# Taking the filler matmuls out of the TensorE stream of a four-stage vision tower

## The chip, the cores and the metric

The kernel runs on one core of one Trainium2 chip. The metric is the time of one execution on the device in microseconds (us); the median of the runs shown counts. A core has TensorE (PE, matrix products; its weight loads are listed as PEld), VectorE (DVE), ScalarE (ACT), GpSimd (POOL) and a queue of transfers issued by SyncE (SP). Engines work in parallel, each through its own list of instructions in order, and wait for each other by semaphores.

## The reference, cut to what matters

64 images of 3 x 224 x 224 are cut into 14 x 14 = 196 patches, and each patch becomes a token of 256 numbers. Four stages follow, each added to its input and then normalised over the 256 numbers.

```python
h = tok(x, W, b)                          # (64, 196, 256): patches times a matrix
h = layernorm(h + mamba(h))               # in-projection, 4 taps, x-projection, scan over tokens, out-projection
h = layernorm(h + rwkv_channel_mix(h))    # r, k, v products of h mixed with its previous token
h = layernorm(h + attention(h))           # 8 heads, leaky scores, softmax, gamma * out + x
h = layernorm(h + top2_moe(h))            # 8 experts, the two best gates of each token
```

Inside the second stage, for 512 channels and 16 states, the scan is `state[t] = dA[t] * state[t-1] + u[t] * B[t]` and the output is the sum over states of `state * C`. All is computed in 32-bit floats.

## The kernel before, in words

The kernel is a software pipeline over images. Work on one image is cut into pieces, and each piece has a slot number (the constants `AT_...`, lines 58 to 141) counted in units of a sixteenth of an image. One pass `step(b, par)` goes through 16 slots g; at each slot every engine does the pieces whose number is g modulo 16, for the image that is there at the time (`live`, line 168). So pieces of about eight images lie side by side at any time, and an image period is 16 slots. Each engine's own `step` function fixes the order within a slot. The order is written out by hand, and no planner changes it.

A slot has a group of the scan as its regular load. GpSimd makes `u * B` for four states (line 474), VectorE scans them in two halves (line 1105) with the decays that ScalarE makes by an exponential (line 907), GpSimd multiplies by C (line 484), and TensorE adds the four states into the bank YB by transposing them (`sum_states`, line 601). After four groups ScalarE drains columns 0 to 255 of YB into `ysb` (line 914). The products `X` go through a ring of six buffers.

Around that load lies the work of the other stages. What the prediction's steps touch:

- TensorE, `project_in` (line 578): the in-projection into the bank pair S, half of it for `z` (slot 20) and half for `xb` (slot -23).
- TensorE, `project_out` (lines 622 and 625), `queries_keys` (line 658), `scores` (line 670), `turn_probs` (line 680), `mix_values` (line 693): the out-projection and the attention.
- TensorE, `expert_pair` (line 721) with the bias row (line 727): two experts at a time, from the scaled inputs `hg` that VectorE makes (line 1221) into a ring of two buffers. The third scaling waits until the first pair is through.
- VectorE, `add_residual` (line 1230): adds the token's input to the experts' sum; it runs once per image.
- VectorE, `attended` (line 1164 and on) after each value product; the gated z (line 1095) and the gated x (line 1090), which free the bank pair S.
- ScalarE: drains of `ysb`, of the transposed probabilities `pT` (line 986), of queries and keys `qm`, `km` (lines 961, 963).
- GpSimd: the inverse deviations of the normalisations (lines 489 to 496).

Among these pieces TensorE also has filler work: `keep_busy(n)` (line 545) issues n products of the identity with a part of the in-projection's weights. They write to columns 256 to 451 of YB, which nothing drains. They wait for no semaphore and raise none. The tuples `AT_WARM` and `WARM` (lines 58 and 59) say at which slots they come and how many: four at slot 5, four at 8, four at 9, three at 12, two at 13, so 17 per image. In the trace each of the products is two records, because a product of 32-bit floats runs in two passes: 34 records per image, 2176 in all.

Of the kernel before, what the change touches and what calls it, by code (L numbers as in the profile page):

```python
# [11 lines left out]
P = 128  # L12
# [5 lines left out]
T = SIDE * SIDE  # L18
BLK = 2
TB = T // BLK  # L20
# [34 lines left out]

AT_WARM = (5, 8, 9, 12, 13,)
WARM = (4, 4, 4, 3, 2,)
AT_LOAD = -39  # L60
AT_PATCH = (-30, -29, -26,)
AT_PATCH_OUT = (-29, -28, -25,)
# [105 lines left out]
def live(b, par, g, slot):  # L168

    if (slot - g) % GROUPS:  # L170
        return ()
    s = image_of(b, slot)
    if isinstance(s, int) and not 0 <= s < IMAGES:
        return ()
    return ((s, (par - slot // GROUPS) % CYCLE),)
# [19 lines left out]
def vit_tower(nc, x, w_tok, b_tok, w_in, conv_w, conv_b, w_xproj, a_log, d_par, dt_w, dt_b, w_out, ln_g, ln_b,  # L195
              w_r, w_k, w_v, mu_r, mu_k, w_qk, b_q, b_k, w_vv, b_v, gamma, w_g, b_g, w_e, b_e,
              ident, q_mask, k_mask, rank_of, proj, gates, out):
    with ExitStack() as ctx:  # L198
        def sb(name, shape, dt=F32):
            return ctx.enter_context(nc.sbuf_tensor(name, shape, dt))  # L200

        def psum(name, shape):
            return ctx.enter_context(nc.psum_tensor(name, shape, F32))
# [7 lines left out]
        win = sb("win", [P, DC, 2 * INNER])  # L211
# [29 lines left out]
        idn = sb("idn", [P, P])  # L241
# [62 lines left out]
        YB = psum("YB", [P, 512])  # L304
# [232 lines left out]
        def _(pe):  # L537
            mm = nc.tensor.matmul
# [3 lines left out]
                after(pe, bank.drained, bank.count(name, s) - 1)  # L542
                return bank.tile

            def keep_busy(n):

                for _ in range(n):
                    mm(YB[0:TB, BLK * P:BLK * P + T], lhsT=idn[:, 0:TB], rhs=win[:, 0, 0:T], start=False, stop=False,  # L548
                       skip_group_check=True)

            def patches(s, part):

                o = free(f"patch{part}", s)
                if part == 0:
                    pe.wait_ge(x_landed, 16 * PATCH * (s + 1))
                for i, col in enumerate(range(QA * part, min(QA * (part + 1), SIDE))):
                    last = nc.tensor.transpose(o[:, i * PROWS:(i + 1) * PROWS], px[:, col, :, :].rearrange("r p w -> r (p w)"),
                                               idn[:PROWS, :PROWS])
                last.then_inc(where[f"patch{part}"].filled, 1)
# [46 lines left out]
            def turn_y(s):  # L606
                pe.wait_ge(normed["y"], s + 1)
                o = free("turn_y", s)
                for c in range(IC):
                    for k in range(BLK):  # L610
                        at = (c % 2) * T + k * TB
                        last = nc.tensor.transpose(o[:, c // 2, at:at + TB], ysb[:, k, c * P:(c + 1) * P],
                                                   idn[:TB, :TB])
                last.then_inc(S.filled, 1)
# [14 lines left out]
            def turn(s, name, src):  # L629
                o = free(name, s)  # L630
                for m in range(DC):
                    for k in range(BLK):
                        last = nc.tensor.transpose(o[:, m * T + k * TB:m * T + (k + 1) * TB],
                                                   src[:, k, m * P:(m + 1) * P], idn[:TB, :TB])
                last.then_inc(where[name].filled, 1)
# [61 lines left out]
            def gate(s, q):  # L697
                pe.wait_ge(where["h3T"].drained, where["h3T"].count("h3T", s))
                o = free("gate", s)
                for k in range(BLK):  # L700
                    for c in range(DC):
                        last = mm(o[0:TB, k * EXPERTS:(k + 1) * EXPERTS], lhsT=h3T[q % 2][:, c, k * TB:(k + 1) * TB],
                                  rhs=wg[:, c, :], start=(c == 0), stop=(c == DC - 1))
                last.then_inc(where["gate"].filled, 1)

            def turn_gates(s):
                pe.wait_ge(where["gate"].drained, where["gate"].count("gate", s))
                o = free("ws", s)
                for k in range(BLK):
                    last = nc.tensor.transpose(o[0:EXPERTS, k * TB:(k + 1) * TB], gw[:, k, :], idn[:TB, :TB])  # L710
                last.then_inc(where["ws"].filled, 1)
# [19 lines left out]
            def turn_moe(s):  # L731
                pe.wait_ge(accT_ready, s + 1)
                o = free("moeT", s)
                for k in range(BLK):
                    for m in range(DC):
                        last = nc.tensor.transpose(o[0:TB, k * D + m * P:k * D + (m + 1) * P],  # L736
                                                   accT[:, m, k * TB:(k + 1) * TB], idn[:])
                last.then_inc(where["moeT"].filled, 1)

            def step(b, par):  # L740
                for g in range(GROUPS):
                    def at(slot):
                        return live(b, par, g, slot)

                    for s, q in at(AT_WARM[0]):
                        keep_busy(WARM[0])
                    for s, q in at(AT_WARM[4]):
                        keep_busy(WARM[4])
                    for s, q in at(AT_H3T):
                        pe.wait_ge(normed["att"], s + 1)  # L750
                        turn(s, "h3T", h3)
                    for s, q in at(AT_WARM[1]):
                        keep_busy(WARM[1])
                    for s, q in at(AT_WARM[2]):
                        keep_busy(WARM[2])
                    for s, q in at(AT_H3T2):
                        turn(s, "h3T2", h3)
                    for s, q in at(AT_TURN_Y):
                        turn_y(s)
                    for s, q in at(AT_WS):  # L760
                        turn_gates(s)
                    for s, q in at(AT_GATE):
                        gate(s, q)
                    for s, q in at(AT_WARM[3]):
                        keep_busy(WARM[3])
                    for p in range(PAIRS):
                        for s, q in at(AT_PAIR[p]):
                            expert_pair(s, p)
                    for s, q in at(AT_MOE_T):
                        turn_moe(s)  # L770
                    for s, q in at(AT_EMBED):
                        embed(s)
                    for s, q in at(AT_V):
                        pe.wait_ge(ksq_ready, s + 1)
                        token_major(s, "v", ka, wv)
                    for part in range(3):
                        for s, q in at(AT_PATCH[part]):
                            patches(s, part)
                    for n in range(UNITS):
                        for s, q in at(AT_SCORES[n]):  # L780
                            scores(s, n)
                    for n in range(UNITS):
                        for s, q in at(AT_TURN_P[n]):
                            turn_probs(s, n)
                    for s, q in at(AT_RK):
                        pe.wait_ge(mix_step, 4 * (s + 1))
                        token_major(s, "r", xr, wr)
                        mix_keys(s)
                    for n in range(UNITS):
                        for s, q in at(AT_AV[n]):  # L790
                            mix_values(s, q, n)
                    for s, q in at(AT_H1T):
                        pe.wait_ge(where["out"].drained, where["out"].count("out", s))
                        turn(s, "h1T", h1)
                    for s, q in at(AT_QK):
                        queries_keys(s)
                    for k in range(GROUPS):
                        for s, q in at(k + 2):
                            sum_states(s, q, k)
                    for s, q in at(AT_Z):  # L800
                        project_in(s, hT[q], "z", IC)
                    for s, q in at(AT_XB):
                        pe.wait_ge(where["embed"].drained, where["embed"].count("embed", s))
                        project_in(s, hT[q], "xb", 0)
                    for s, q in at(AT_XPROJ):
                        xproj(s)
                    for s, q in at(AT_OUT):
                        project_out(s, q)
                    for s, q in at(AT_H2T):
                        pe.wait_ge(normed["ffn"], s + 1)  # L810
                        turn(s, "h2T", h2[q % 2])
                    for s, q in at(AT_VALUES):
                        token_major(s, "values", h2T, wvv)
# [568 lines left out]
```

## Time and profile before

| | us |
|---|---|
| median of the three runs | 5296.42 |
| range of the three runs | 5291.37 to 5298.24 |
| profiled execution, span from the first to the last instruction | 5291.6 |
| busy in the profiled execution: TensorE | 4820.6 |
| VectorE | 3739.1 |
| ScalarE | 3911.0 |
| GpSimd | 4452.7 |

The profile gives no other time for its execution than the span. It is read as follows: the busy time of an engine is the union of its instructions, and ends of TensorE's records are modelled, since products are pipelined. The granted clock of TensorE stands as a share of 2.4 GHz; it has two levels, 0.50 (1.2 GHz) and 1.00 (2.4 GHz), and a figure between them is a mean over a stretch that has both. In a timeline, consecutive records of one line are merged; a bracket tells how long the engine stood idle before the first of them, and what ended that.

### The profile page before, as it was taken

How to read it: one execution, taken by the hardware profiler on the slowest of the kernel's cores; microseconds unless marked ns; L12 is line 12 of the kernel's file. 1: busy time of each engine (PE TensorE's matmuls, PEld its weight loads, DVE VectorE, ACT ScalarE, POOL GpSimd, SP SyncE). 2: the span in 40 equal slices, each digit the busy share in tenths (PEclk: the TensorE clock that was granted, in tenths of full speed). 3: DMA queues.
4: the chain of work that ended last, by engine and by line, in shares of the span. 5: the costliest groups of instructions: out<-in, count | busy, mean ns of one | idle time of the engine just before them, and what ended most of it. 6: DMA issues, size and time to landing. Idle time of an engine off the chain costs nothing. (4 is left out here: it accounts for less than half of the span.)

```text
span 5291.6 us, 96290 instructions
## 1 busy us (share of the span) xinstructions
PE 4820.6 (91%) x33664; PEld 4234.3 (80%) x33664; DVE 3739.1 (71%) x7504; ACT 3911.0 (74%) x9282; POOL 4452.7 (84%) x3336
## 2 busy tenths in 40 slices
PE   4789999999999999999999999999999999999986
PEld 4678888888888888888888888888888888888776
DVE  3567777777777777777777777777777777777653
ACT  4687787787777787777777777787777777777751
POOL 4998898898898898898888888898898898898840
PEclk8899999999999999999999999999999999999986
DMA  4222222222222222222222222222222322322200
GB/s 96 60 54 71 57 61 72 57 62 72 61 61 68 59 66 66 64 63 64 67 60 64 68 59 64 67 61 64 71 59 61 71 59 61 75 58 58 66 16 25
DMA packets 730625, 329.04 MB, mean 62 GB/s; under 512 B 631542, under 2 KB 655392, under 8 KB 729888
## 3 DMA queue, kind: packets, MB, share of 16 engines
q1 hardware_dynamic: 730144, 322.89, 25.0%
q8 instruction: 269, 4.41, 0.3%
q14 instruction: 212, 1.74, 0.1%
HBM read 307.88 MB, written 14.90 MB: 61 GB/s over the span
## 5 line engine op out<-in xcount | busy, mean ns | idle before, releaser
L1105 DVE TENSOR_TENSOR_SCAN X<-dA,X 128x392 f32<-128x392 f32 x2048 | 1871.4, 955 | 844.9 <-POOL X L474 447.9
L474 POOL TENSOR_TENSOR X<-u,Bb 128x784 f32<-128x784 f32 x1024 | 1898.2, 1854 | 3.9 <-DMA Bb<-proj_rows 3.9
L484 POOL TENSOR_TENSOR X<-X,Cb 128x784 f32<-128x784 f32 x1024 | 1897.2, 1853 | 1.1 <-DVE X L1105 1.1
L907 ACT ACTIVATE dA<-dt,negA 128x195 f32<-128x195 f32 x4096 | 1511.6, 417 | 135.2 <-DVE X L1105 116.2
L601 PE MATMUL YB<-idn,X 128*98 128x128 f32 x8192 | 1106.7, 281 | 25.6 <-POOL X L484 25.4
L601 PEld LDWEIGHTS YB<-idn,X 128*98 128x98 f32 x8192 | 931.3, 132 | 62.9 <-POOL X L484 33.9
L721 PE MATMUL G<-hg,we 128*128 128x196 f32 x4096 | 727.8, 334 | 27.1 <-DVE hg L1221 27.1
L721 PEld LDWEIGHTS G<-hg,we 128*128 128x128 f32 x4096 | 694.9, 194 | 47.4 <-issue 40.8
L578 PE MATMUL SB<-hT,win 128*128 128x196 f32 x2048 | 375.3, 337 | 58.0 <-ACT pT L986 55.8
L548 PE MATMUL YB<-win,idn 128*98 128x196 f32 x2176 | 424.1, 335 | 0.0
L693 PEld LDWEIGHTS G<-vs,pT 98*98 98x98 f32 x4096 | 392.6, 171 | 36.2 <-issue 33.4
L693 PE MATMUL G<-vs,pT 98*98 98x33 f32 x4096 | 397.8, 253 | 21.0 <-DVE ob L1119 9.2
L578 PEld LDWEIGHTS SB<-hT,win 128*128 128x128 f32 x2048 | 340.1, 192 | 84.5 <-issue 66.2
L978 ACT ACTIVATE pr<-pr,nmx 98x196 f32<-98x196 f32 x1024 | 382.6, 447 | 8.2 <-DVE nmx L1152 2.6
L1082 DVE SCALAR_TENSOR_TENSOR xbs<-SB,cw,xbs 128x195 f32<-128x195 f32 (+2 forms) x768 | 266.8, 409 | 166.9 <-ACT xbs L851 162.7
L489 POOL TENSOR_TENSOR veps_att<-mv_att,epsc 98x2 f32<-98x2 f32 x64 | 12.6, 197 | 435.0 <-DVE mv_att L1114 435.0
L1221 DVE TENSOR_TENSOR hg<-G,Gb 128x784 f32<-128x784 f32 x256 | 241.4, 963 | 179.8 <-PE G L721 167.1
L914 ACT ACTIVATE ysb<-YB 98x256 f32<-98x256 f32 x256 | 96.1, 375 | 355.6 <-PE YB L601 345.4
L548 PEld LDWEIGHTS YB<-win,idn 128*98 128x98 f32 x2176 | 350.1, 169 | 3.2
L670 PE MATMUL SB<-km,qm 32*98 32x392 f32 x1024 | 235.0, 533 | 104.8 <-DVE xbs L1090 100.3
L569 PE MATMUL G<-patT,wtok 128*128 128x196 f32 x1536 | 277.2, 338 | 4.3 <-ACT patT L833 4.2
L680 PE MATMUL SB<-idn,pr 98*98 98x98 f32 x2048 | 219.7, 251 | 66.2 <-DVE zs L1095 62.5
(149 smaller groups left out, 7609.0 us busy)
## 6 DMA issues: line engine op xcount, KB each, us to landing
Bb<-proj_rows SPq DMA_DIRECT2D x256, 392.0 KB, 5.2
Cb<-proj_rows SPq DMA_DIRECT2D x256, 392.0 KB, 4.1
Gb<-gate_rows SPq DMA_DIRECT2D x64, 784.0 KB, 5.5
px<-in_x SPq DMA_DIRECT2D x1024, 36.8 KB
out<-ob SPq DMA_DIRECT2D x64, 196.0 KB
dtin<-proj_rows SPq DMA_DIRECT2D x64, 98.0 KB, 2.8
we<-in_w_e SPq DMA_DIRECT2D x1, 2048.0 KB
proj_rows<-pj SPq DMA_DIRECT2D x64, 25.3 KB
```

The source lines that it names most:

```text
L474: tt(X[(GROUPS * s + g) % RING][:], u[q % 2][:, c:c + 1, :].broadcast_to([P, NG, T]), Bb[:, NG * ng:NG * (ng + 1), :], ALU.mult).then_inc( ...
L484: tt(t[:], t[:], Cb[:, n0:n0 + NG, :], ALU.mult).then_inc(prod_ready, 1)
L548: mm(YB[0:TB, BLK * P:BLK * P + T], lhsT=idn[:, 0:TB], rhs=win[:, 0, 0:T], start=False, stop=False, skip_group_check=True)
L569: last = mm(o[:, m * T:(m + 1) * T], lhsT=wtok[:, k, m * P:(m + 1) * P], rhs=patT[:, half * COLORS + c, :], start=(k == 0), stop=(k == KP ...
L578: last = mm(o[:, j // 2, (j % 2) * T:(j % 2 + 1) * T], lhsT=win[:, k, m * P:(m + 1) * P], rhs=src[:, k, :], start=(k == 0), stop=(k == DC ...
L601: last = mm(YB[0:TB, k * P:(k + 1) * P], lhsT=X[(GROUPS * s + g) % RING][:, j, k * TB:(k + 1) * TB], rhs=idn[:], is_transpose=True, start= ...
L693: last = mm(o[0:TB, j * (DV + 1):(j + 1) * (DV + 1)], lhsT=pT[:, j // 2, at:at + TB], rhs=vs[q % 2][:, k, h0 + j, :], start=(k == 0), stop ...
L721: last = mm(o[:, m * T:(m + 1) * T], lhsT=we[:, k, at:at + P], rhs=hg[p % GRING][:, e, k, :], start=(p == 0 and e == 0 and k == 0 and m == 0),
L907: last = go(dA[i % DRING][:, j, 1:T], dt_[q % 2][:, c, 1:T], ACT.Exp, scale=negA[:, c, n:n + 1])
L978: last = go(pr[i % PRING][:, j, :], pr[i % PRING][:, j, :], ACT.Exp, bias=nmx[i % PRING][:, j:j + 1])
L1082: last = v.scalar_tensor_tensor(out=xbs[:, c, k:], in0=S.tile[:, c // 2, at:at + T - k], scalar=cw[:, c, TAPS - 1 - k:TAPS - k], in1=xbs[: ...
L1105: v.tensor_tensor_scan(t, dA[i % DRING].rearrange("p n t -> p (n t)"), t, 0.0, ALU.mult, ALU.add).then_inc(scan_done, 1)
```

## The change

The filler products go: their function, their five calls and the two tuples. Every other piece keeps its slot and its place in the order of its engine.

```diff
-AT_WARM = (5, 8, 9, 12, 13,)
-WARM = (4, 4, 4, 3, 2,)
...
-            def keep_busy(n):
-
-                for _ in range(n):
-                    mm(YB[0:TB, BLK * P:BLK * P + T], lhsT=idn[:, 0:TB], rhs=win[:, 0, 0:T], start=False, stop=False,
-                       skip_group_check=True)
-
...
-                    for s, q in at(AT_WARM[0]):
-                        keep_busy(WARM[0])
-                    for s, q in at(AT_WARM[4]):
-                        keep_busy(WARM[4])
                     for s, q in at(AT_H3T):
                         pe.wait_ge(normed["att"], s + 1)
                         turn(s, "h3T", h3)
-                    for s, q in at(AT_WARM[1]):
-                        keep_busy(WARM[1])
-                    for s, q in at(AT_WARM[2]):
-                        keep_busy(WARM[2])
...
                     for s, q in at(AT_GATE):
                         gate(s, q)
-                    for s, q in at(AT_WARM[3]):
-                        keep_busy(WARM[3])
```

## Rows read from the trace of the kernel before

**Rows 1.** The page: busy us, share and instructions of engines; granted clock in 40 slices.

```profile
PE 4820.6 (91%) x33664; PEld 4234.3 (80%) x33664; DVE 3739.1 (71%) x7504; ACT 3911.0 (74%) x9282; POOL 4452.7 (84%) x3336
...
PEclk8899999999999999999999999999999999999986
```

**Rows 2.** Instructions of L1230 in four stretches: duration ns, first and last start us.

```profile
L1230 DVE TENSOR_TENSOR accT<-G,h3T x5: 554/555/556, 1062.6 to 1377.5; 128x392 f32<-128x392 f32 x5
...
L1230 DVE TENSOR_TENSOR accT<-G,h3T x58: 553/555/557, 429.0 to 4940.6; 128x392 f32<-128x392 f32 x58
...
L1230 DVE TENSOR_TENSOR accT<-G,h3T x2: 554/555/556, 1456.3 to 1536.7; 128x392 f32<-128x392 f32 x2
...
L1230 DVE TENSOR_TENSOR accT<-G,h3T x2: 554/555/556, 1536.7 to 1616.3; 128x392 f32<-128x392 f32 x2
```

**Rows 3.** Stretches: us; busy us of PE, PEld, DVE, ACT, POOL; PEclk, DMA share, GB/s.

```profile
1117.00:1196.00 79.00, 73.49 (x531) 64.56 (x530) 58.55 (x118) 61.24 (x147) 69.80 (x53) 1.00 0.26 64
...
485.00:4909.00 4424.00, 4142.31 (x29392) 3647.41 (x29393) 3256.97 (x6532) 3408.79 (x8110) 3887.75 (x2908) 0.99 0.26 64
```

**Rows 4.** Groups by line: busy us, mean ns of one, idle us before them.

```profile
L548 PE MATMUL YB<-win,idn 128*98 128x196 f32 x2176 | 424.1, 335 | 0.0
```

**Rows 5.** Timeline of PE, one undisturbed image: start us, us, what, idle before.

```profile
1200.70 0.83 PE L548 MATMUL YB<-win,idn 128*98 128x196 f32 x4
1201.95 5.54 PE L721 MATMUL G<-hg,we 128*128 128x196 f32 x32 [0.43 <-DVE hg L1221]
...
1240.25 1.49 PE L548 MATMUL YB<-win,idn 128*98 128x196 f32 x8
...
1243.14 0.85 PE L680 MATMUL SB<-idn,pr 98*98 98x98 f32 x8 [0.96 <-DVE zs L1095]
...
1255.43 1.49 PE L548 MATMUL YB<-win,idn 128*98 128x196 f32 x8
1256.76 1.50 PE L693 MATMUL G<-vs,pT 98*98 98x33 f32 x16
...
1259.32 1.49 PE L548 MATMUL YB<-win,idn 128*98 128x196 f32 x8
...
1262.80 2.89 PE L578 MATMUL SB<-hT,win 128*128 128x196 f32 x16 [1.11 <-ACT pT L986]
...
1274.54 1.16 PE L548 MATMUL YB<-win,idn 128*98 128x196 f32 x6
1277.34 0.90 PE L670 MATMUL SB<-km,qm 32*98 32x392 f32 x4 [1.65 <-DVE xbs L1090]
```

**Rows 6.** Timelines of VectorE, GpSimd and ScalarE, same image: waits for TensorE and behind.

```profile
1204.88 0.97 DVE L1221 TENSOR_TENSOR hg<-G,Gb 128x784 f32<-128x784 f32 x1 [2.19 <-PE G L721]
...
1206.99 0.20 POOL L489 TENSOR_TENSOR veps_att<-mv_att,epsc 98x2 f32<-98x2 f32 x1 [6.08 <-DVE mv_att L1114]
...
1245.43 0.18 DVE L1164 RECIPROCAL rg<-G 98x4 f32<-98x4 f32 x1 [0.42 <-PE G L693]
...
1272.37 0.92 ACT L961 ACTIVATE qm<-G,bqm,qmask 96x196 f32<-96x196 f32 x2 [4.14 <-PE G L658]
```

**Rows 7.** Two stretches (columns of rows 3), and the timeline of PE in the second.

```profile
1481.80:1488.60 6.80, 6.72 (x34) 5.92 (x33) 6.07 (x26) 6.26 (x17) 6.72 (x6) 0.50 0.02 5
...
1594.40:1597.80 3.40, 3.40 (x18) 2.77 (x15) 3.33 (x7) 1.80 (x5) 1.82 (x2) 0.51 0.36 118
...
1597.37 1.08 PE L548 MATMUL YB<-win,idn 128*98 128x196 f32 x4
1598.28 4.97 PE L721 MATMUL G<-hg,we 128*128 128x196 f32 x29
```

**Rows 8.** Timeline of PE in the last images, and the stretch around (columns of rows 3).

```profile
5116.20 1.51 PE L680 MATMUL SB<-idn,pr 98*98 98x98 f32 x8
5119.21 2.85 PE L693 MATMUL G<-vs,pT 98*98 98x33 f32 x16 [1.50 <-DVE ob L1119]
...
5115.00:5125.00 10.00, 7.59 (x36) 6.53 (x37) 3.40 (x14) 2.87 (x6) 2.69 (x3) 0.50 0.30 102
```

## The prediction, made before the change was run

> **What bounds the kernel now.** First the page's engine line and its clock line [rows 1]: TensorE (PE) is busy for 91% of the span, more than any other engine, and its granted clock reads 9 tenths or more from the third of the 40 slices to the third from the end. The share alone would say that PE is the bound and that less work on it is time won. So the next look is at one instruction that runs once per image, the residual add of line 1230 [rows 2]. Its starts give the length of an image: (1377.5 - 1062.6) / 4 = 78.73 us in an undisturbed stretch, and (4940.6 - 429.0) / 57 = 79.15 us over all 57 steady intervals. A whole image is 57 times in the sum below; the difference of 0.42 us per image, 24 us in all, is to be explained too.
>
> In the undisturbed stretch the clock is 1.00, that is 2.4 GHz, and PE is busy 73.5 of 79 us [rows 3]. The fillers take 424.1 us of the span and no idle time stands before them [rows 4]. What PE does behind each filler is in its timeline over one image [rows 5]. There are five groups: 4 records at 1200.70, 8 at 1240.25, 8 at 1255.43, 8 at 1259.32 and 6 at 1274.54. The reader is to see the idle time in brackets: after the fillers, PE stands still and waits for another engine, 0.96 us before L680 (VectorE), 1.11 before L578 (ScalarE), 1.65 before L670 (VectorE) and 0.43 before L721 (VectorE). No filler ends a wait of anybody; at 2.4 GHz each lies beside a wait that PE would have anyway.
>
> The image's length is set by a chain that changes engines. Its PE links are those for which another engine stands idle [rows 6]: the first expert pair (VectorE waits 2.19 us for L721, and GpSimd 6.08 us for the statistics behind that), the probability transposes and value products (VectorE waits for L693), and the long run from L578 at 1262.80 to the query projection (ScalarE waits 4.14 us for L658, until 1272.37: 9.5 us of PE). So PE's idle stretches and PE's chain links lie side by side: every link starts just after one of the four waits of rows 5.
>
> **What the change removes.** Five groups per image, 34 records. One record steps by 166 ns: the group of 8 at 1255.43 is followed by the next work at 1256.76 [rows 5], 1.33 us later. That is 34 x 0.166 = 5.6 us of PE time per image, and I cost it at zero gain: the waits on ScalarE and VectorE that follow hide it, and those engines don't wait for a filler. The same removal lengthens PE's idle time by what stood in front of each wait: before L680 from 0.96 to about 2.3 us, before L578 from 1.11 to 3.8 us (two groups, less what the work between them can use), before L670 from 1.65 to 2.65, before L721 from 0.43 to 1.1. Nothing else is removed: no wait, no semaphore, no DMA; the queues of SP and GpSimd are untouched, since the fillers carry no increment and write columns 256 to 451 of YB, which no drain reads.
>
> **What it costs.** The clock falls to 1.2 GHz behind such idle stretches already, fillers and all [rows 7]: in 1481.8 to 1488.6 it is 0.50 (behind the wait before L680), in 1594.4 to 1597.8 0.51 (behind the wait before L670). These falls come in some images only. The image from 1536.7 to 1616.3, with only the second of them, took 79.6 us, 0.9 more than the undisturbed one; the one from 1456.3 to 1536.7, with falls at both places, 80.4, so 1.7 more [rows 2]. The average over all images is the 0.42. With the idle stretches 1.0 to 2.7 us longer, I expect a fall in nearly every image at each of three places:
>
> - Place 1, L680 and L693 behind the wait for VectorE. In the last images, where the clock was 0.50, the transposes took 1.51 us and the products 2.85 [rows 8], against 0.85 and 1.50 at 2.4 GHz [rows 5]. All of it low costs 0.66 + 1.35 = 2.0 us, a fall that starts behind it nothing. I take the middle, 1.0.
> - Place 2, L578 and what follows, 9.5 us of dense chain work. Rows before show no fall here. The bounds are 0 (the fall ends before 1262.80) and half of a low stretch of 6.8 us, 3.4; the short low stretch of rows 7 (3.4 us) at half speed costs 1.7. I take 1.7, since the work is dense and a fall may start inside the wait.
> - Place 3, L670 to the first expert pair. In the fall of 1594.4 four filler records take 0.91 us [rows 7] instead of 4 x 0.166 = 0.66, after other slowed work, and L721 starts late. Measured: 0.9 per image [rows 2]. Lower bound 0 (the filler's own time goes), upper bound the whole first pair at half speed: half of 5.54 us [rows 5], 2.8. I take 0.9, the nearest row.
>
> Sum 3.6 us per image; with a fall nine times in ten at each, 3.24. Of this 0.42 is paid already: 2.8 x 57 = 160 us. The start and the drain already run at a lower clock [rows 1] and get no term. The profiled execution spans 5291.6 us, at the low end of the runs shown (5291.4 to 5298.2, median 5296.4), so nothing large lies around it and 5 us are added to come to the median: 5291.6 + 160 + 5 = **5457 us**.
>
> The Trainium skill, "TensorE: Matmul & The Clock Gate", section Terms, prices time at the low clock as that time times one minus the granted share, so half of it. The trace disagrees for this kernel: the image that starts at 1456.3 was low for 6.8 us at place 1 [rows 7] and fell at place 3 as well, 10.2 us if that fall is as long as the one of 1594.4, which gives 5.1 us, and the image was 1.7 longer, because much of the low time lay beside other engines' work. By that rule three low stretches of 3.4 us would make 5.1 us per image.
>
> **Rivals.**
> (a) Only the two places that already fall do so, now in every image; place 2 keeps its clock. For: no row shows a fall there. Against: its idle stretch becomes the longest of all. 1.0 + 0.9 - 0.42 = 1.48, times 57: 84 us, so 5380 us.
> (b) The clock holds about as it does now, and the change does nothing. For: PE remains busy for about 68 of 79 us, and the undisturbed stretch holds 1.00 [rows 3] with waits of up to 1.65 us in it [rows 5]. Against: the falls of rows 7 came behind waits that the fillers still kept short. 5296 us, up to 5349 if the falls become a few more: 53 us, 0.9 per image, is place 3 alone in every image. The Trainium skill's same page, Part 1, says that the ramp penalty is under 1% of a typical kernel's span; by that, too, the change would stay under 5349 us. The trace so far agrees (24 us of 5292), but in a kernel with the fillers in.
> (c) Faster: the fillers themselves are what a fall costs. Mechanism: at 1.2 GHz the filler group at place 3 stands between L601 and L721; it begins at 1597.37 and L721 at 1598.28, 0.91 us later [rows 7], about the 0.9 that the image lost. Without it L721 starts on time, and if the falls don't become more frequent, up to 24 us come back: 5273 us. It decides while falls at place 2 (1.7 us each) come in fewer than 24 / 1.7 = 14 of the 57 images; below 8 of them the gain is over 0.2%. Against: the longer idle stretches before that place.
> (d) Every low stretch is paid in full, as chain work is dense at all three places and the clock needs as long to come back as before. 3 x 1.7 - 0.42 = 4.7, times 57: 267 us, so 5563 us. For: with fillers gone the cover of rows 5 is thin. Against: the 1.7 us that 10.2 low ones cost. By the rule of the skill's section Terms this would be the case.
>
> **How the numbers follow.** Forecast (three places, most images, 5381 to 5540) 0.67; (a) 0.14; (b) 0.08, of which 0.05 ends within the bound and 0.03 above it; (c) 0.04; (d) 0.07. About 0.2%, 10.6 us, is what a measurement of this kernel can tell from no change. Faster 0.04, the same 0.05, slower 0.67 + 0.14 + 0.03 + 0.07 = 0.91. The range takes in (a) with some of its spread and ends just short of (d): 5360 to 5550 us. The bounds of the places alone (0 to 2.0, 0 to 3.4, 0 to 2.8) would reach from no cost to 8.2 us per image; falls at the outer ends of all three at once I leave out.
>
> **What would show it.** Right: line 548 is gone; the residual add comes every 81 to 83 us instead of 78.7; the steady granted clock falls from 0.99 to about 0.9 to 0.95; L578, L693 and L721 show records near double length in most images; the idle time before L670 and L578 is longer in full-clock images; ScalarE waits longer than 4.14 us for L658 in a good part of the images. Each place is right if its own fall is there and the engine behind it waits longer by its term. Wrong: the interval stays at 78.7 to 79.2 with the clock at 0.99, (b); falls at places 1 and 3 only, (a); falls as now but no lost 0.9 at place 3, (c); an interval over 83.5, (d). Should the clock fall and the interval stay, the chain as I read it is wrong.

## The result, and the profile after

| | before | after |
|---|---|---|
| median, us | 5296.39 | 5461.04 |
| range of four runs, us | 5291.37 to 5298.24 | 5456.63 to 5464.29 |
| span of the profiled execution, us | 5291.6 | 5454.8 |

The ratio of after to before is 1.0312, with a 95% interval of 1.0297 to 1.0326: the change costs 165 us. The prediction was 5457 us.

Lines move up in the changed file: L578 is L570 after, L601 is L593, L622 is L614, L658 is L650, L670 is L662, L680 is L672, L693 is L685, L721 is L713, L961 is L943, L1230 is L1212.

First the page of the changed kernel, its engine line and its clock line, which answer to [rows 1].

```profile
PE 4681.1 (86%) x31488; PEld 4110.7 (75%) x31488; DVE 3741.5 (69%) x7504; ACT 3915.2 (72%) x9282; POOL 4447.5 (82%) x3336
...
PEclk7889999999999999999999999999999999999987
```

TensorE lost 2176 records and 139.5 us of busy time, and the kernel is longer. At one digit the clock line shows almost nothing of the cause. The residual add shows it, over all steady images and over four of them (answers to [rows 2]).

```profile
L1212 DVE TENSOR_TENSOR accT<-G,h3T x58: 552/556/558, 433.7 to 5103.0; 128x392 f32<-128x392 f32 x58
...
L1212 DVE TENSOR_TENSOR accT<-G,h3T x5: 552/555/558, 1089.0 to 1416.7; 128x392 f32<-128x392 f32 x5
```

(5103.0 - 433.7) / 57 = 81.92 us per image, against 79.15, and (1416.7 - 1089.0) / 4 = 81.93 in the sample. Before, 39 of the 57 images had no fall of the clock and took some 78.7 us, and the others up to 80.8; now every image has a fall, and 45 of the 57 lie within 0.1 us of 81.92. 57 x 2.77 = 158 us of the 163 us by which the span grew lie here; 4.7 us come before the first of these adds (433.7 against 429.0).

Then stretches of the changed kernel, with the columns of [rows 3]: the steady part, the two stretches of one image in which the clock was low, and the one around L662 and L713.

```profile
485.00:5070.00 4585.00, 4030.33 (x27541) 3550.08 (x27540) 3265.05 (x6548) 3415.11 (x8115) 3886.31 (x2910) 0.94 0.25 61
...
2015.30:2018.60 3.30, 3.30 (x21) 3.15 (x19) 2.69 (x15) 2.84 (x7) 3.16 (x4) 0.50 0.01 2
2032.30:2039.10 6.80, 6.06 (x18) 5.92 (x19) 3.13 (x6) 4.17 (x11) 6.80 (x5) 0.50 0.79 85
2047.40:2059.20 11.80, 8.06 (x54) 7.10 (x53) 7.89 (x16) 5.37 (x14) 5.16 (x5) 1.00 0.20 68
```

The timeline of TensorE in that image (answers to [rows 5]) tells what ran there.

```profile
2013.17 0.85 PE L672 MATMUL SB<-idn,pr 98*98 98x98 f32 x8 [2.29 <-DVE zs L1077]
2013.86 1.50 PE L685 MATMUL G<-vs,pT 98*98 98x33 f32 x16
2015.19 1.87 PE L593 MATMUL YB<-idn,X 128*98 128x128 f32 x8
2016.85 1.51 PE L604 MATMUL SB<-idn,ysb 98*128 98x98 f32 x8
...
2029.14 0.53 PE L625 MATMUL G<-idn,h 98*128 98x98 f32 x4 [0.98 <-ACT wsT L1016]
...
2033.04 5.57 PE L570 MATMUL SB<-hT,win 128*128 128x196 f32 x16 [2.49 <-ACT pT L968]
2038.40 2.28 PE L614 MATMUL G<-wout,y 128*98 128x256 f32 x8
...
2044.01 1.55 PE L650 MATMUL G<-h2T,wqk 128*96 128x196 f32 x8
...
2050.56 0.90 PE L662 MATMUL SB<-km,qm 32*98 32x392 f32 x4 [2.64 <-DVE xbs L1072]
...
2053.92 5.54 PE L713 MATMUL G<-hg,we 128*128 128x196 f32 x32 [1.09 <-DVE hg L1203]
```

Four things are to be seen. The waits grew (2.29, 2.49, 2.64 and 1.09 us, against 0.96, 1.11, 1.65 and 0.43), at places 1 and 3 by what the fillers had filled; before L570 only by 1.38 us, and another 0.98 stands before L625. At place 1 the transposes and the value products still run at 2.4 GHz (0.85 and 1.50 us), and the short fall hits the work behind them, L593 and L604. At place 2 the whole projection L570 takes 5.57 us instead of 2.89. At place 3, where the wait is the longest in this list, nothing falls: L713 takes 5.54 us as before.

Over the 57 images, place 1 falls in all, place 2 in 55 and place 3 in 2. One of the two images without a fall at place 2, by the residual add and the projection:

```profile
L1212 DVE TENSOR_TENSOR accT<-G,h3T x2: 557/557/557, 2402.7 to 2481.6; 128x392 f32<-128x392 f32 x2
...
2445.58 2.89 PE L570 MATMUL SB<-hT,win 128*128 128x196 f32 x16 [1.93 <-ACT pT L968]
```

Its clock is low at place 1 alone, for 6.8 us; its projection takes 2.89 us, and the image 78.9. So in one and the same kernel an image with the fall at place 2 is 3.0 us longer than one without it.

Last the waits of other engines in the image of the long timeline above (timelines of VectorE, GpSimd and ScalarE, answers to [rows 6]).

```profile
2056.85 0.97 DVE L1203 TENSOR_TENSOR hg<-G,Gb 128x784 f32<-128x784 f32 x1 [2.19 <-PE G L713]
...
2058.96 0.19 POOL L487 TENSOR_TENSOR veps_att<-mv_att,epsc 98x2 f32<-98x2 f32 x1 [6.64 <-DVE mv_att L1096]
...
2045.59 0.91 ACT L943 ACTIVATE qm<-G,bqm,qmask 96x196 f32<-96x196 f32 x2 [5.13 <-PE G L650]
```

VectorE waits for the expert pair exactly as long as before; ScalarE waits 1 us longer for the query projection.

### The profile page after: what moved, and what is told of

The parts are those of the page before. It is cut to its first block and busy times, and to the rows that moved or that the text cites. A ratio compares the mean times of both kernels' runs of the same rounds, so it can differ in the third digit from the quotient of the medians.

```text
span 5454.8 us, 91938 instructions
## 1 busy us (share of the span) xinstructions
PE 4681.1 (86%) x31488; PEld 4110.7 (75%) x31488; DVE 3741.5 (69%) x7504; ACT 3915.2 (72%) x9282; POOL 4447.5 (82%) x3336
## 5 line engine op out<-in xcount | busy, mean ns | idle before, releaser
L593 PE MATMUL YB<-idn,X 128*98 128x128 f32 x8192 | 1137.2, 286 | 27.6 <-POOL X L482 27.6
L593 PEld LDWEIGHTS YB<-idn,X 128*98 128x98 f32 x8192 | 952.0, 134 | 63.2 <-POOL X L482 35.7
L713 PE MATMUL G<-hg,we 128*128 128x196 f32 x4096 | 729.8, 335 | 73.0 <-DVE hg L1203 73.0
L713 PEld LDWEIGHTS G<-hg,we 128*128 128x128 f32 x4096 | 693.7, 194 | 92.5 <-DVE att L1151 81.3
L570 PE MATMUL SB<-hT,win 128*128 128x196 f32 x2048 | 526.0, 429 | 150.3 <-ACT pT L968 148.1
L570 PEld LDWEIGHTS SB<-hT,win 128*128 128x128 f32 x2048 | 478.0, 255 | 178.3 <-issue 160.0
L685 PE MATMUL G<-vs,pT 98*98 98x33 f32 x4096 | 402.1, 254 | 23.6 <-DVE ob L1101 12.1
L685 PEld LDWEIGHTS G<-vs,pT 98*98 98x98 f32 x4096 | 392.8, 173 | 38.8 <-issue 35.9
L662 PE MATMUL SB<-km,qm 32*98 32x392 f32 x1024 | 232.4, 528 | 165.0 <-DVE xbs L1072 160.0
L672 PE MATMUL SB<-idn,pr 98*98 98x98 f32 x2048 | 219.5, 251 | 147.2 <-DVE zs L1077 143.6
L672 PEld LDWEIGHTS SB<-idn,pr 98*98 98x98 f32 x2048 | 188.2, 129 | 167.0 <-issue 163.4
L943 ACT ACTIVATE qm<-G,bqm,qmask 96x196 f32<-96x196 f32 x128 | 58.4, 505 | 325.4 <-PE G L650 325.4
```

What stands on the lines that cost most here:

```text
L570: last = mm(o[:, j // 2, (j % 2) * T:(j % 2 + 1) * T], lhsT=win[:, k, m * P:(m + 1) * P], rhs=src[:, k, :], start=(k == 0), stop=(k == DC ...
L593: last = mm(YB[0:TB, k * P:(k + 1) * P], lhsT=X[(GROUPS * s + g) % RING][:, j, k * TB:(k + 1) * TB], rhs=idn[:], is_transpose=True, start= ...
L672: last = nc.tensor.transpose(o[0:TB, j // 2, at:at + TB], pr[(UNITS * s + n) % PRING][:, j, k * TB:(k + 1) * TB], idn[:TB, :TB])
L685: last = mm(o[0:TB, j * (DV + 1):(j + 1) * (DV + 1)], lhsT=pT[:, j // 2, at:at + TB], rhs=vs[q % 2][:, k, h0 + j, :], start=(k == 0), stop ...
L713: last = mm(o[:, m * T:(m + 1) * T], lhsT=we[:, k, at:at + P], rhs=hg[p % GRING][:, e, k, :], start=(p == 0 and e == 0 and k == 0 and m == 0),
```

## The experiments

Image lengths below are differences of the residual add's starts in each run's own trace, over 57 steady images where no stretch is named. Falls are counted in the same images: a fall is a stretch in which the clock is 0.50.

**Fillers at place 2 only.** The slots are 5, 8, 9, 12 and 13.

```diff
-WARM = (4, 4, 4, 3, 2,)
+WARM = (0, 4, 4, 0, 0,)
```

> Fillers only at slots 8 and 9, ahead of place 2 (the xb projection, L578 and on); none at slots 5, 12, 13. After the change each image had a long low stretch over the xb projection and a short one behind place 1, and none at place 3, at 81.92 us per image. Theory A (the cost is the clock at place 2): the projection stays at 2.4 GHz, most of the 165 us is back, and what is left is at place 1, 79 to 80 us per image: 5300 to 5370 us. Rival B (the three places share the cost, as the prediction had it; place 3 was spared only because the fall at place 2 shifted the image): falls at places 1 and 3 come back, 80.5 to 81.5 us per image: 5390 to 5450 us. Rival C (the fillers help by their time in PE's order, not by the clock): two of five groups back, 5395 us, with no link to the granted clock.

Measured: 5441.98 us, ratio 1.0276 (1.0260 to 1.0291), steady clock 0.93. Theory A falls and B holds: the place that carried the whole loss in the changed kernel is covered again, and only 19 us come back. The loss moved. The timeline of TensorE in this run:

```profile
3180.96 0.90 PE L670 MATMUL SB<-km,qm 32*98 32x392 f32 x4 [2.65 <-DVE xbs L1090]
...
3184.32 8.13 PE L721 MATMUL G<-hg,we 128*128 128x196 f32 x32 [0.76 <-DVE hg L1221]
```

A stretch of that time with the columns of [rows 3], its clock 0.52:

```profile
3182.50:3189.40 6.90, 6.14 (x23) 5.74 (x22) 2.48 (x6) 3.31 (x9) 0.57 (x1) 0.52 0.17 52
```

And the residual add over 11 images:

```profile
L1230 DVE TENSOR_TENSOR accT<-G,h3T x12: 555/556/558, 2795.5 to 3696.6; 128x392 f32<-128x392 f32 x12
```

Now place 3 falls, in 49 of the 57 images, beside place 1 in all of them: the two expert pairs take 8.13 us instead of 5.54. The wait before it is 2.65 us, the same as the 2.64 of the changed kernel, where the clock stayed at 1.00. So the length of the wait alone doesn't decide. The image is (3696.6 - 2795.5) / 11 = 81.92 us in this stretch, the length of the changed kernel, with the long fall at another place; over all 57 images it is 81.48.

**No fillers at place 2.**

```diff
-WARM = (4, 4, 4, 3, 2,)
+WARM = (4, 0, 0, 3, 2,)
```

> Fillers at slots 5, 12 and 13 as before, none at slots 8 and 9. Theory A: the xb projection runs low in nearly every image and the time is near that of the changed kernel, 5410 to 5465 us. Rival B: only place 2's own share is paid, 1.7 us per image by the prediction, 5296 + 97 = 5393 us or less. Rival C: three of five groups kept, 5365 us.

Measured: 5447.48 us, ratio 1.0287 (1.0271 to 1.0302), 81.65 us per image. Here theory A's number comes out and B's does not. Its timeline of TensorE shows the same long fall as the changed kernel has, and the wait at place 3 as in the kernel before:

```profile
2927.00 5.56 PE L578 MATMUL SB<-hT,win 128*128 128x196 f32 x16 [2.50 <-ACT pT L986]
...
2944.49 0.90 PE L670 MATMUL SB<-km,qm 32*98 32x392 f32 x4 [1.65 <-DVE xbs L1090]
...
2947.85 5.54 PE L721 MATMUL G<-hg,we 128*128 128x196 f32 x32 [0.43 <-DVE hg L1221]
```

Place 2 falls in 54 of the 57 images; place 1 falls in 37 and place 3 in 15, though their fillers are there. With the run before: opening place 2 costs 152 us, opening places 1 and 3 costs 147, opening all three 165. The losses don't add.

**Fillers over 8 partitions.**

```diff
-mm(YB[0:TB, BLK * P:BLK * P + T], lhsT=idn[:, 0:TB], rhs=win[:, 0, 0:T], start=False, stop=False,
+mm(YB[0:TB, BLK * P:BLK * P + T], lhsT=idn[0:8, 0:TB], rhs=win[0:8, 0, 0:T], start=False, stop=False,
```

> All fillers stay in their slots with the same count, output and length (196 columns, 98 output rows), but multiply over 8 partitions instead of 128. Theory A (clock): PE is busy as before, record for record, at equal clock; if the short products do as much for the clock as the full ones, 5296 us, and if they do little, the clock falls as in the changed kernel and the time is 5400 to 5500 us; either way time and granted clock go together. Rival C (their time in PE's order helps): 5296 us whatever the clock is.

Measured: 5652.54 us, ratio 1.0674 (1.0656 to 1.0692), 85.18 us per image, steady clock 0.90. The fillers' place in TensorE's order is the same as before, and the kernel is the slowest of all, so it isn't their time in the order that helps; rival C is out. From this run, the timeline of TensorE in one image:

```profile
3042.01 2.93 PE L548 MATMUL YB<-win,idn 8*98 8x196 f32 x8
...
3046.60 4.37 PE L578 MATMUL SB<-hT,win 128*128 128x196 f32 x16
...
3065.97 1.62 PE L548 MATMUL YB<-win,idn 8*98 8x196 f32 x4
3067.51 8.57 PE L721 MATMUL G<-hg,we 128*128 128x196 f32 x32
```

The stretch of this image, with the columns of [rows 3]:

```profile
3000.70:3088.50 87.80, 85.16 (x528) 74.32 (x526) 58.41 (x119) 61.09 (x146) 69.72 (x53) 0.86 0.24 58
```

With these fillers TensorE is busy for 85.16 of 87.8 us and still the clock is 0.86; and a group that takes 1.49 us at full clock takes 2.93 and then stands in front of chain work. That fits the 191 us more than with no fillers at all: where fillers don't hold the clock, they are ordinary work at half speed. How much of the 191 us it accounts for, no run shows.

**Every group doubled.**

```diff
-WARM = (4, 4, 4, 3, 2,)
+WARM = (8, 8, 8, 6, 4,)
```

> Every filler group doubled. By the prediction's reading the groups cost nothing because PE waits behind them: 0.96 us before L680, 1.11 before L578, 1.65 before L670, 0.43 before L721 at full clock. Doubling adds 1.33, 2.66, 1.00 and 0.66 us there, so it overruns by 0.4 + 1.5 + 0 + 0.2 = 2.1 us per image and ends the falls (0.42): 5296 + 57 x (2.1 - 0.42) = 5392 us, with clock 1.00 in the steady part. Rival (fillers were on the chain all along): doubling costs all of their 5.6 us per image, 5296 + 320 = 5616 us. Rival (much more slack than read): 5270 us.

Measured: 5352.50 us, ratio 1.0109 (1.0094 to 1.0124), steady clock 1.00, no low stretch in 57 images, 80.21 us per image: 1.5 us of overrun where 2.1 were expected, so the time lies 40 us under the 5392 of the expectation. The slack is where it was read. Of the groups by line of this run, the idle time before L578 and L680 (58.0 and 66.2 us in the kernel before) has nearly gone:

```profile
L578 PE MATMUL SB<-hT,win 128*128 128x196 f32 x2048 | 368.3, 333 | 3.7 <-ACT hT L842 1.7 <-ACT pT L986 1.3
...
L680 PE MATMUL SB<-idn,pr 98*98 98x98 f32 x2048 | 218.2, 250 | 6.0 <-ACT pr L971 2.7 <-DVE zs L1095 2.3 <-ACT pT L986 0.8
```

**More fillers at places 1 and 3 only.**

```diff
-WARM = (4, 4, 4, 3, 2,)
+WARM = (6, 4, 4, 6, 2,)
```

> Against the kernel before: six fillers instead of four at slot 5 (ahead of L680) and six instead of three at slot 12 (ahead of L670); 0.66 and 1.0 us more of PE per image, into waits of 0.96 and 1.65 us. Theory (a fall of the clock comes behind the idle stretches, and fillers within the wait are free): no fall in the steady part, every image 78.7 us as in the undisturbed stretch, 5296 - 24 = 5272 us. Rival (longer fillers sit on the chain): 57 x 1.66 = 95 us more, 5390 us, or something between. Rival (0.42 per image is not the clock): 5296 us.

Measured: 5266.51 us, ratio 0.9950 (0.9937 to 0.9963), 78.77 us per image. The theory's number was 5272. This version beats both kernels, by 28 us and 195 us. The residual add over the steady images:

```profile
L1230 DVE TENSOR_TENSOR accT<-G,h3T x58: 554/556/558, 425.7 to 4915.3; 128x392 f32<-128x392 f32 x58
```

The steady stretch, with the columns of [rows 3]:

```profile
485.00:4880.00 4395.00, 4176.90 (x29913) 3679.37 (x29911) 3254.59 (x6525) 3403.44 (x8100) 3878.71 (x2903) 1.00 0.26 64
```

The longer group at slot 5 and the wait behind it, from the timeline of TensorE:

```profile
1233.47 2.15 PE L548 MATMUL YB<-win,idn 128*98 128x196 f32 x12
1236.37 0.85 PE L680 MATMUL SB<-idn,pr 98*98 98x98 f32 x8 [0.31 <-DVE zs L1095]
```

The longer group leaves 0.31 us of the 0.96, and the clock of the steady part is 1.00: none of the 57 images has a fall. So the 0.42 us per image of the kernel before were falls, and covered waits cost nothing.

**Chain work added, with and without falls.** In the kernel with more fillers and in the changed kernel, one operation of GpSimd whose result nobody reads, behind the statistics of the attention norm; a second version for the changed kernel is smaller.

```diff
                 if n in shift:
                     pool.wait_ge(rstd_step[n], steps * (s + 1))
                     tt(shift[n][:], shift[n][:], rstd[n][:], ALU.mult).then_inc(shifted[n], 1)
+                if n == "att":
+                    tt(pad[:], bv[:], bv[:], ALU.add)
```

In the smaller version the line is `tt(pad[:, 0:2], bv[:, 0:2], bv[:, 0:2], ALU.add)`. From the groups by line of GpSimd, the changed kernel with the larger operation (which takes 614 ns in the kernel with more fillers, too) and with the smaller:

```profile
L497 POOL TENSOR_TENSOR pad<-bv 98x256 f32<-98x256 f32 x64 | 39.3, 614 | 0.0
```

```profile
L497 POOL TENSOR_TENSOR pad<-bv 98x2 f32<-98x2 f32 x64 | 12.4, 193 | 0.0
```

> The kernel with more fillers, and one added product-free GpSimd operation per image (98 x 256 numbers, about 0.6 us by the 392-wide one at 0.84) right behind the statistics of the attention norm, on the chain. Without falls the image has to grow by its whole length: 78.7 + 0.6 = 79.3 us, 57 x 0.6 = 34 us more than the kernel with more fillers, 5306 us. If GpSimd is not on the chain there: no difference.

Measured: 5306.80 us, 40.3 more than without the operation; 64 x 0.614 = 39.3. No image has a fall. The operation is on the chain, and where no clock falls the chain takes it in full.

> The changed kernel with the same added GpSimd operation. Theory E (in the changed kernel the image length is held by the falls: a longer image moves the next fall against the work, and the falls give way): the image stays at 81.9 us, 5461 us, within 8 us, although 0.6 us of chain work was added. Rival S (the length is a sum of prices): 82.5 us per image, 5461 + 34 = 5495 us.

Measured: 5502.82 us, 41.8 more than the changed kernel. Theory E falls in this form: the 0.61 us are paid. But the images are no longer even. The residual add over one image each, at two places of this run:

```profile
L1215 DVE TENSOR_TENSOR accT<-G,h3T x2: 555/556/556, 3243.5 to 3330.1; 128x392 f32<-128x392 f32 x2
...
L1215 DVE TENSOR_TENSOR accT<-G,h3T x2: 556/556/557, 3494.4 to 3574.8; 128x392 f32<-128x392 f32 x2
```

That is 86.6 us and 80.4 us, in sequences that partly repeat, with 82.72 on average: two or three falls per image, at places that change from image to image.

> The changed kernel with a smaller added GpSimd operation at the same place (98 x 2 numbers, about 0.2 us by the lines of the inverse deviations). With 0.61 us the images lost their even length. Theory E in a weaker form (the falls give way for a small shift): 81.9 us per image as before, 5461 us within 5. Rival S: 57 x 0.2 = 11 us more, 5472 us or more, and uneven images if the falls lose their place.

Measured: 5458.69 us, 2.4 less than the changed kernel at a spread of some 4, although 57 x 0.193 = 11 us of chain work was added. The residual add over five images of this run:

```profile
L1215 DVE TENSOR_TENSOR accT<-G,h3T x6: 554/555/557, 683.5 to 1093.1; 128x392 f32<-128x392 f32 x6
```

(1093.1 - 683.5) / 5 = 81.92 us. Of the 57 images 38 lie within 0.1 us of that, the others between 79.0 and 84.7, and the mean is 81.95. Where the 0.19 us went, the trace shows in a later image of even length (1994.3 to 2076.2):

```profile
2037.37 5.56 PE L573 MATMUL SB<-hT,win 128*128 128x196 f32 x16 [2.50 <-ACT pT L971]
2042.72 2.02 PE L617 MATMUL G<-wout,y 128*98 128x256 f32 x8
...
2048.08 1.55 PE L653 MATMUL G<-h2T,wqk 128*96 128x196 f32 x8
```

From the start of the projection to the end of L653 it is 2048.08 + 1.55 - 2037.37 = 12.26 us, where the changed kernel takes 12.52 (L650 there): L617 at first takes 2.02 us instead of 2.28, so the fall takes less of the work. The rest of the image is longer by as much, the operation included. So this shift was absorbed in most images, and the larger one was not. It is one run of each size; how the falls find their place, and why the larger shift breaks the even length, stays open.

**Fillers as transposes.**

```diff
-WARM = (4, 4, 4, 3, 2,)
+WARM = (6, 6, 6, 5, 3,)
...
-mm(YB[0:TB, BLK * P:BLK * P + T], lhsT=idn[:, 0:TB], rhs=win[:, 0, 0:T], start=False, stop=False,
+mm(YB[0:TB, BLK * P:BLK * P + P], lhsT=idn[:, 0:TB], rhs=idn[:], is_transpose=True, start=False, stop=False,
```

> Fillers of the kernel before as transposes: the identity turned, 128 columns each, 6, 6, 6, 5 and 3 of them, so about the same columns per group (768 for 784, 640 for 588, 384 for 392). Theory (what holds the clock is array work of any kind over all partitions): 5296 us, clock 0.97. Rival (a transpose does not count for the clock, as the Trainium skill, TensorE: Matmul & The Clock Gate, Part 4, has it): falls as with no fillers or with short ones, 5460 to 5650 us, clock 0.92 or less.

Measured: 5330.27 us, ratio 1.0058 (1.0038 to 1.0078), steady clock 0.98, 79.48 us per image. The five runs are uneven: two at 5310.5 us and three at 5330 to 5336, and the profile, with its clock and its image length, is of one of the former. The result lies between, much nearer the first: 36 us over the kernel before, where no fillers cost 165. But the groups are not as long as the expectation made them. In the trace a product of a filler is two records and a transpose one (1664 for 64 images with 26 transposes):

```profile
L548 PE MATMUL YB<-idn 128*98 128x128 f32 x1664 | 246.9, 282 | 0.0
```

```profile
1240.92 0.82 PE L548 MATMUL YB<-idn 128*98 128x128 f32 x6
...
1243.79 0.85 PE L680 MATMUL SB<-idn,pr 98*98 98x98 f32 x8 [1.62 <-DVE zs L1095]
```

A group takes 0.82 us instead of 1.49, and the wait behind it is 1.62 us instead of 0.96. The Trainium skill's page "TensorE: Matmul & The Clock Gate", Part 4, says that a transpose doesn't count as busy in the same way for the clock. This run disagrees in the main: with groups of transposes of about half the length, place 2 falls in none of the 57 images and 19 have no fall at all, where without fillers place 2 fell in 55 and every image had a fall. Whether a transpose does less for the clock than a product of the same length isn't parted here from the shorter groups: either can be what the 36 us are.

**One place opened at a time.**

```diff
-WARM = (4, 4, 4, 3, 2,)
+WARM = (0, 4, 4, 3, 2,)
```

> The kernel before without the four fillers at slot 5, ahead of L680 (place 1); all other fillers stay. In the runs so far the kernels with falls in every image all came to 81.5 to 81.9 us per image, whichever places fell, and one place was enough when it was place 2. Theory M (prices of falls don't add; one open place brings most of the loss): over 5400 us. Rival S (each place has a price of its own; place 1's is the smallest, 0.2 to 1.2 us per image): 5300 to 5360 us.

Measured: 5357.94 us, ratio 1.0116 (1.0099 to 1.0133), 80.27 us per image, clock 0.96. (The kernel with fillers over 8 partitions, at 85.18 us, does not fit the 81.5 to 81.9 of this expectation.) In 25 of the 57 images the only fall is one of 6.8 us at place 1, and they take some 80.3 us; in 29 place 3 falls too, though it has its fillers. An image of the first kind:

```profile
L1230 DVE TENSOR_TENSOR accT<-G,h3T x2: 554/555/556, 995.3 to 1075.7; 128x392 f32<-128x392 f32 x2
...
1019.19 2.77 PE L693 MATMUL G<-vs,pT 98*98 98x33 f32 x16
```

The image takes 80.4 us. Here the fall begins 23.6 us behind the residual add, over the value products, and costs 1.6 us; in the image of 78.9 us of the changed kernel it began 25.6 us behind it, after those products, was as long, and cost 0.2. So what a fall costs depends on the work that it meets.

```diff
-WARM = (4, 4, 4, 3, 2,)
+WARM = (4, 4, 4, 0, 0,)
```

> The kernel before without the fillers at slots 12 and 13, around L670 and ahead of the first expert pair (place 3); all other fillers stay. Theory M: over 5400 us. Rival S: 0.9 us per image by the prediction, less what is paid now, 5296 + 57 x 0.5 = 5325 us, and at most 5296 + 57 x 2.4 = 5433 us with the whole first pair low.

Measured: 5366.89 us, ratio 1.0116 (1.0077 to 1.0156), clock 0.95. Theory M falls in both: a single open place costs 61 or 70 us, where place 2 costs 152. Rival S gives the size for place 1 (within its range) and is low for place 3 (70 against 29, within its bound of 137). One run of four of the last kernel took 5323.75 us and three 5364 to 5370; the trace of one of the slower ones suggests why: the residual add over five early and ten later images.

```profile
L1230 DVE TENSOR_TENSOR accT<-G,h3T x6: 553/554/556, 670.7 to 1080.2; 128x392 f32<-128x392 f32 x6
...
L1230 DVE TENSOR_TENSOR accT<-G,h3T x11: 554/555/557, 2864.3 to 3661.9; 128x392 f32<-128x392 f32 x11
```

The images are (1080.2 - 670.7) / 5 = 81.90 us first and (3661.9 - 2864.3) / 10 = 79.76 later, of one and the same program: two patterns of falls within one execution. That the run of 5323.75 us had more of the second is not shown, since it has no trace.

## Why the prediction was right, and which of its steps were not

**The chain and the zero gain: right.** Fillers inside a wait are free: the version with more fillers loses nothing by them, and doubling all groups costs 1.5 us per image, once the waits are overrun. That the chain runs through L578 to L658 shows directly. L658 in the undisturbed image of [rows 5]:

```profile
1270.78 1.55 PE L658 MATMUL G<-h2T,wqk 128*96 128x196 f32 x8
```

From the start of the projection to the end of L658 it was 1270.78 + 1.55 - 1262.80 = 9.53 us, and it is 2044.01 + 1.55 - 2033.04 = 12.52 after. That is 2.99 of the 3.19 us by which an image exceeds the undisturbed 78.73. The other 0.2 lies between the residual add and the projection (42.9 us for 42.7), and nothing lies behind L658.

**The kind of cost: right.** The clock falls behind the lengthened waits and the chain pays. The fillers over 8 partitions rule out the other reading, that they help by their time.

**The sum by places: wrong in its parts.** The working gave 1.0 + 1.7 + 0.9 = 3.6 us, nine tenths of it 3.24; the image grew by 3.19. Place 2 was mis-sized: its low stretch is 6.8 us, not 3.4, the projection alone costs 5.57 - 2.89 = 2.68, and with L614 the place costs 2.99 where 1.7 was taken (the bound given was 3.4). The wait before it became 2.49 us, not the 3.8 that the prediction read. Place 1 has its fall in every image, but behind the chain's link, so it costs 0.2 where 1.0 was taken. The trace before had that price: the image from 2961.7 to 3040.6 has a fall at place 1 alone, for 3.4 us, and takes 78.9 us.

```profile
L1230 DVE TENSOR_TENSOR accT<-G,h3T x2: 555/556/556, 2961.7 to 3040.6; 128x392 f32<-128x392 f32 x2
```

Place 3 costs next to nothing where 0.9 was taken, since it falls in 2 of 57 images. The start, which got no term, cost 4.7 us. The errors of the places cancel (0.2 + 2.99 for 3.24), and that the time came within 4 us is luck in good part.

**The step that failed** is "a fall in nearly every image at each of three places": it treated the falls as independent. They aren't: with place 2 covered and the others open, place 3 falls and the kernel takes nearly as long (5442 us); with only place 3 open it costs 70 us. Whether a place falls depends on more than its wait, as 2.64 and 2.65 us show, with the clock at 1.00 in one kernel and a fall in the other. What else decides it was not isolated.

**The rivals.** (a), falls at places 1 and 3 only, is contradicted: place 2 falls in 55 of 57 images and place 3 in 2. (b) is contradicted. The Trainium skill's "TensorE: Matmul & The Clock Gate", Part 1, gives its 1% for the ramp, that is the warm-up of a kernel. Taken for falls in the steady part, as the prediction took it, it fits the kernel with its fillers (24 of 5292 us) and not the one without (165 of 5296 us, 3.1%). (c), faster, is contradicted: it asked for falls at place 2 in fewer than 14 images, and there were 55. That fillers at half clock can stand in front of chain work shows in another kernel, the one over 8 partitions. (d), every low stretch paid in full, is contradicted: an image of the changed kernel has low stretches of 3.4 and 6.8 us, and the first costs 0.2 us, since it meets little chain work; 3.19 us are paid for both. By the Trainium skill's "TensorE: Matmul & The Clock Gate", section Terms, they would cost 5.1 us.

**What the prediction wanted to see.** The interval of 81 to 83 us and the clock of 0.9 to 0.95 came (81.92 and 0.94), so did the double length of L578 and ScalarE's longer wait (5.13 for 4.14 us); the double length of L693 and L721 didn't come (1.50 and 5.54 us in the image shown, as before).

## What to carry to other kernels

Work on an engine with idle stretches isn't priced by its busy time: look at what it stands in front of, and then at the granted clock in a stretch, not at its mean (one digit hid a loss of 3%). Cover waits that lie ahead of chain work with array work that fits inside them, and check by the image length, not by the fillers' count: two groups made a little longer gave 28 us, doubling all of them cost 57. When several places can lose the clock, take them out one by one and all together, since what one costs depends on the others, and on the work that its fall meets.

## What was not expected of the hardware

Kernels with falls at different places come to the same 81.92 us, within 0.1, in most of their images: the changed one in 45 of 57 and the one with the small added operation in 38 (falls at places 1 and 2), the one with fillers at place 2 alone in 38 (places 1 and 3). In the changed one the falls stand at the same point of the image to some 0.3 us in nearly all of them. An added 0.19 us per image vanished in it; 0.61 us broke it up into images of 80.4 to 86.6 us. Why this length, no run shows. Products over 8 partitions left the clock at 0.86 in an image in which TensorE was busy for 97% of the time; transposes over 128 partitions, in groups of about half the length, held it nearly as products did (0.98 for 0.99).
